# Two-layer transformer kernel on one core: the second attention's q and k projected once, the rotary partner fetched by transfers

## What is computed

```python
def rotate_half(x):
    half = x.shape[-1] // 2
    x1, x2 = (x[..., :half], x[..., half:])
    return jnp.concatenate([-x2, x1], axis=-1)

def apply_rope(x, base=BASE):
    ...
    emb = jnp.concatenate([freqs, freqs], axis=-1)
    return x * jnp.cos(emb) + rotate_half(x) * jnp.sin(emb)

q = (x @ q_w.T + q_b).reshape(B, S, H, Dh).transpose(0, 2, 1, 3)
k = (x @ k_w.T + k_b).reshape(B, S, H, Dh).transpose(0, 2, 1, 3)
q = apply_rope(q)
k = apply_rope(k)
attn = jnp.einsum('bhqd,bhkd->bhqk', q, k) * scaling
```

## Time and profile before

| | |
|---|---|
| time, median of 3 runs (lowest to highest) | 868.04 us (867.67 to 874.63) |
| span of the profiled execution | 863.3 us |
| the profiled execution's own time | not recorded; the median is 4.7 us above the span |
| TensorE busy | 828.1 us (96%), 4549 matmuls |
| VectorE, ScalarE, GpSimd busy | 646.3 (75%), 525.3 (61%), 465.8 us (54%) |
| granted TensorE clock, mean | 0.994 |
| projections of q and k, layer 1 | 96 matmuls, 493 to 623 us |

### The profile page before, as it was taken

The page is one execution under the profiler, slowest core; times in us unless marked ns, Lnnn a source line. Parts: engine busy times, 40 slices in busy tenths (PEclk is TensorE's granted clock), DMA queues, the critical chain, the costliest instruction groups (busy, mean ns, idle before and its releaser), DMA issues.

```text
span 863.3 us, 14805 instructions
## 1 busy us (share of the span) xinstructions
PE 828.1 (96%) x4549; PEld 627.4 (73%) x4549; DVE 646.3 (75%) x1350; ACT 525.3 (61%) x1106; POOL 465.8 (54%) x399
## 2 busy tenths in 40 slices
PE   8899999999989999989998999999999999999997
PEld 6678788777878888766887887764444447888886
DVE  5898888999998888998376865868788634676553
ACT  3778788787867888863644533336576554454442
POOL 4565555666665556551666776623300426656774
PEclk9999999999999999999999999999999989999999
DMA  4222222322422223122665357412441132334442
GB/s 157 93 98 87 98 97 97 106 81 87 152 74 99 98 97 110 61 69 60 208 210 182 131 163 275 138 57 73 137 136 51 57 99 93 123 123 142 152 162 65
DMA packets 57426, 99.20 MB, mean 115 GB/s; under 512 B 8272, under 2 KB 19024, under 8 KB 57360
## 3 DMA queue, kind: packets, MB, share of 16 engines
q1 hardware_dynamic: 57360, 98.39, 34.3%
HBM read 71.88 MB, written 9.57 MB: 94 GB/s over the span
## 4 chain that ended last, share of the span: by engine, by line
PE 64%; issue 10%; POOL 10%; DVE 10%; ACT 4%; DMA 2%; SPq 0%; DVEq 0%; POOLq 0%; ACTq 0%
PE ps L974 10%; PE ps L951 10%; PE ps L960 9%; PE ps L319 6%; PE ps L382 5%; PE ps L330 4%; POOL q_sin L526 3%; PE ps L343 3%; PE ps L370 3%; PE ps L1642 2%; PE ps L1523 2%; PE ps L357 2%; PE ps L1612 2%; POOL wqk_lo L513 2%; DVE nm L1834 2%
## 5 line engine op out<-in xcount | busy, mean ns | idle before, releaser
L1098 POOL TENSOR_TENSOR ew_lo<-ew_raw,ew_hi 128x768 fp32r<-128x768 f32 x68 | 128.6, 1892 | 56.7 <-ACT ew_hi L1064 48.5
L1050 ACT ACTIVATE hid_hi<-guw 128x512 fp32r<-128x512 f32 x68 | 43.0, 632 | 156.2 <-POOL guw L1114 106.2
L1153 DVE TENSOR_TENSOR hid_lo<-guw,hid_hi 128x512 fp32r<-128x512 f32 x68 | 78.9, 1160 | 72.4 <-ACT hid_hi L1050 72.3
L1114 POOL TENSOR_TENSOR guw<-gu,cwb 128x512 f32<-128x512 f32 x61 | 80.4, 1318 | 92.4 <-issue 76.4
L526 POOL TENSOR_TENSOR q_sin<-q_sw,sin 128x512 f32<-128x512 f32 x64 | 83.5, 1312 | 51.7 <-DMA q_sw<-q_in 50.4
L1834 DVE TENSOR_REDUCE nm<-ps 128x1 f32<-128x512 f32 x128 | 81.4, 683 | 19.0 <-PE ps L1546 17.8
L1729 ACT ACTIVATE e<-ps 128x512 f32<-128x512 f32 x128 | 68.7, 602 | 35.6 <-PE ps L1642 35.3
L974 PE MATMUL ps<-ew_hi,hid_hi 128*128 128x256 f32 x272 | 78.3, 288 | 2.4 <-DVE hid_lo L1153 1.8
L505 DVE SCALAR_TENSOR_TENSOR w<-ex,rden,sgn 128x512 f32<-128x512 f32 (+3 forms) x128 | 79.0, 680 | 0.0
L433 ACT ACTIVATE ex<-sabs,nmax 128x512 f32<-128x512 f32 (+3 forms) x128 | 61.5, 551 | 28.1 <-DVE nmax L479 28.1
L974 PE MATMUL ps<-ew_lo,hid_hi 128*128 128x256 f32 x272 | 76.8, 282 | 0.0
(11 more groups left out here) (189 smaller groups left out, 2401.6 us busy)
## 6 DMA issues: line engine op xcount, KB each, us to landing
ew_raw<-in_ew SPq DMA_DIRECT2D x68, 384.0 KB, 3.3
q_sw<-q_in SPq DMA_DIRECT2D x128, 128.0 KB, 2.0
cwb<-cw_dram SPq DMA_DIRECT2D x61, 256.0 KB, 3.7
wqk_raw<-in_wqk SPq DMA_DIRECT2D x32, 256.0 KB, 2.6
wv_raw<-in_wv SPq DMA_DIRECT2D x32, 128.0 KB, 2.4
wo_raw<-in_wo SPq DMA_DIRECT2D x32, 128.0 KB, 2.2
qs<-stk_q SPq DMA_DIRECT2D x16, 256.0 KB, 3.5
ks<-stk_k SPq DMA_DIRECT2D x16, 256.0 KB, 4.1
```

The source lines that it names most:

```text
L1098: pool.tensor_tensor(ff[f].ew[1][:, i % EW_SLOTS, :], ew_raw[:, i % RAW_SLOTS, :], fp(ff[f].ew[0][:, i % EW_SLOTS, :]), ALU.subtract).then ...
L1114: pool.tensor_tensor(ff[f].guw[:, i % 2, :], ff[f].gu[:, i % 2, :], ff[f].cwb[:, r % CWB_SLOTS, :], ALU.mult).then_inc(sem("guw"), 1)
L1153: dve.tensor_tensor(ff[f].hid[1][:, i % 2, :], ff[f].guw[:, i % 2, :], fp(ff[f].hid[0][:, i % 2, :]), ALU.subtract).then_inc(sem("hid_lo"), 1)
```

## The change

The plain weights alone are loaded, split and used: 48 projection matmuls instead of 96. The split of a weight writes the channels of a head in another order, the two halves interleaved, so that a channel and its rotary partner are neighbouring rows. Scores are sums over a head's channels, so the order is free as long as q and k share it. The tables and biases are loaded with the same order.

For each group ScalarE now evicts the projection with its bias (`evict`), SP issues two transfers that exchange odd and even rows (`swap_halves`), GpSimd multiplies by the signed sine (`turned`), VectorE makes the cosine part from PSUM after the eviction (`group_dve`), and the sum is made on VectorE in the rows and on GpSimd in the steps (`rotated`). The order of the queues and the places of groups, high halves, stores and loads change with it.

```diff
-        w1_raw = sb("w1_raw", [P, 6, DC, D])
+        w1_raw = sb("w1_raw", [P, 4, DC, D])
...
-        ROW_GROUP = {21: ((0, 0), (0, 1)), 22: ((1, 0), (1, 1)), 23: ((2, 0), (2, 1)), 24: ((3, 0),), 25: ((3, 1),)}
+        ROW_GROUP = {21: 0, 22: 1, 23: 2, 24: 3}
         ROW_V = {25: 0, 26: 1}
-        ROW_HIGH = {22: 0, 23: 1, 24: 2, 26: 3}
+        ROW_HIGH = {22: 0, 23: 1, 24: 2, 25: 3}
...
-        ROW_STACK = {23: 0, 24: 1, 26: 2, 27: 3}
-        ROW_LOADS = {25: (0, 4), 29: (4, SLOTS)}
+        ROW_STACK = {23: 0, 24: 1, 25: 2, 26: 3}
+        ROW_LOADS = {25: (0, 4), 28: (4, SLOTS)}
...
-        STEP_GROUP = {(4, 1): (4, 0), (4, 3): (4, 1), (5, 1): (5, 0), (5, 3): (5, 1), (7, 2): (6, 0), (8, 2): (6, 1),
-                      (9, 3): (7, 0), (10, 3): (7, 1)}
-        STEP_HIGH = {5: 4, 6: 5, 9: 6, 11: 7}
+        STEP_GROUP = {(4, 1): 4, (5, 1): 5, (7, 2): 6, (8, 2): 7}
+        STEP_HIGH = {6: 4, 7: 5, 9: 6, 10: 7}
...
-        W1_AT = {11 + 2 * part: part for part in range(5)}
+        W1_AT = {11 + 2 * part: part for part in range(3)}
...
+        def swap_halves(sp, g):
+            sp.wait_ge(sem("qk1_ev"), g + 1)
+            wait(sp, "rs", g - 1)
+            for o in range(2):
+                sp.dma_start(qw[o:P:2, g % 2, :], qe[1 - o:P:2, g % 2, :]).then_inc(sem(f"qk1_sw{g % 2}"), 16)
...
-            if i in ROW_STACK:
-                stack(sp, ROW_STACK[i])
...
+            if i in ROW_STACK:
+                stack(sp, ROW_STACK[i])
+            if i in ROW_GROUP:
+                swap_halves(sp, ROW_GROUP[i])
...
             loads_after(sp, 0)
+            swap_halves(sp, 4)
+            swap_halves(sp, 5)
             maxima(sp, 2)
             stack(sp, 4)
             stack(sp, 5)
             sp.wait_ge(sem("stk_st"), 16 * 3 * 6)
+            swap_halves(sp, 6)
             loads_after(sp, 1)
+            swap_halves(sp, 7)
             maxima(sp, 3)
             stack(sp, 6)
+            stack(sp, 7)
             loads_after(sp, 2)
-            stack(sp, 7)
             maxima(sp, 4)
...
+        def evict(act, g):
+            t, mt, h = GROUPS1[g]
+            act.wait_ge(sem("qk1_ps"), g + 1)
+            if g == 0:
+                act.wait_ge(sem("tab1"), 16 * 7)
+            wait(act, f"qk1_sw{g % 2}", 32 * (g // 2))
+            act.activation(qe[:, g % 2, :], ps[:, BANK_OF["qk", g], :], ACT.Identity,
+                           bias=b1[:, 2 * t, mt:mt + 1]).then_inc(sem("qk1_ev"), 1)
...
             if i in ROW_HIGH:
                 high(act, ROW_HIGH[i])
+            if i in ROW_GROUP:
+                evict(act, ROW_GROUP[i])
...
+                for j in range(HEADS):
+                    if (s, j) in STEP_GROUP:
+                        evict(act, STEP_GROUP[s, j])
                 if s in STEP_HIGH:
                     high(act, STEP_HIGH[s])
...
+        def turned(pool, g):
+            pool.wait_ge(sem(f"qk1_sw{g % 2}"), 32 * (g // 2 + 1))
+            wait(pool, "rr", g - 1)
+            pool.tensor_tensor(rs[:, g % 2, :], qw[:, g % 2, :], sin1[:, :], ALU.mult).then_inc(sem("rs"), 1)
...
-            if i in ROW_GROUP and ROW_GROUP[i][-1][1] == 1:
-                rotated(pool, ROW_GROUP[i][-1][0])
+            if i in ROW_GROUP:
+                turned(pool, ROW_GROUP[i])
...
             for g in range(4, 8):
+                turned(pool, g)
                 rotated(pool, g)
-                low(pool, g)
+                if g % 2 == 1:
+                    low(pool, g - 1)
+                    low(pool, g)
...
-        def group_dve(dve, g, sw):
+        def group_dve(dve, g):
...
+            dve.wait_ge(sem("qk1_ev"), g + 1)
...
+            dve.scalar_tensor_tensor(out=rc[:, g % 2, :], in0=ps[:, BANK_OF["qk", g], :],
+                                     scalar=b1[:, 2 * t, mt:mt + 1], in1=cos1[:, :],
+                                     op0=ALU.add, op1=ALU.mult).then_inc(sem("qk1_cos"), 1)
...
-                for g, sw in ROW_GROUP.get(i, ()):
-                    group_dve(dve, g, sw)
+                if i in ROW_HIGH:
+                    rotated(dve, ROW_HIGH[i])
+                if i in ROW_GROUP:
+                    group_dve(dve, ROW_GROUP[i])
```

88 lines of the change are left out of this document (47 added, 41 removed).

## The result

The changed kernel takes **875.57 us** (median of 20 runs, 870.74 to 884.02); the kernel before, on the same chip, 867.84 (20 runs, 862.40 to 876.82). The ratio is 1.0095, 95% interval 1.007 to 1.012: **slower by some 8 us**, where 2.7 us less were forecast. The profiled execution took 873.37 us, with a span of 871.2 for 863.3, and a mean granted clock of 0.984 for 0.994.

A forecast was written before the change was run, and what follows sets the result against it. TensorE, 96% busy, was taken as the bound, except for a chain of transfers before step 9. The terms -5.6 + 0.5 - 0.3 + 4.9 - 3.2 + 1.0 = -2.7 us gave a median of 865.3 us, range 858 to 873.

The forecast's parts named there:

- Rows, -5.6: Rows 21 to 24: four swapped projections go from a chain that is TensorE's alone, 4 x 1.40 = -5.6 us.
- What comes in their place, +0.5: Rows 21 to 24: eviction, exchange, sine product and sum run late but mostly covered, +0.5 us, bounds 0 and +2.5.
- The cycle: Rows 21 to 24: evict, swap, product, sum, high half and signalling for one group, 6.4 us against a 5.6 us row.
- the cover: Rows: slack, about 3.6 us, since GpSimd's weighting is used two rows later and gates wait for earlier low halves.
- The chosen bound, +2.5: Rows 21 to 24: the upper bound given for the +0.5 us cost of what replaces the swapped projections.
- Norm, -0.3: Ahead of the norm: fewer weight loads and splits shorten the chain there, -0.3 us, bounds -0.6 and 0.
- Release at step 9, +4.9: Attention steps 4 to 8: later maxima and group 5's store delay the stacked k reload to 619.9 from 614.95, +4.9 us.
- Group 7's projections, -3.2: Attention steps 9 to 13: group 7's two projections go, -3.2 us.
- Load at step 13, +1.0: Quad 2's loads, behind the stores of groups 6 and 7, land late for TensorE: +1.0 us, bounds 0 and +4.
- The rival of the stores: Rows and step 13: swaps and reload wait behind stacked stores, landings over some 6 us; +2.2, 870.2 us, chance 0.20.
- three quarters of TensorE's saving: TensorE loses 12.0 us of work; three quarters of it come back as waiting at steps 9 and 13.
- The 4.7 us: Whole kernel: median run 868.04 us less profiled span 863.3, taken as constant.

The follow-up runs named there:

- no_exchange: The changed kernel without the exchange transfers, the sine multiplying the unexchanged projection (values wrong); 869.79 us, ratio 1.0053 to the kernel before.
- before_loads_late: The kernel before with one edit: the load of the second quad's rows issued behind the store of group 7; 876.06 us, ratio 1.0131.
- no_exchange_early: The changed kernel without exchange transfers, group 5 projected at the end of step 4, second quad's load ahead of group 7's store; 863.3 us, ratio 0.9952.
- combined_swap6: The kernel combined with group 6's exchange put back ahead of the loads and ahead of the wait for the stores; 864.51 us, ratio 0.9987.
- combined: The changed kernel with rows' evictions and exchanges earlier, group 5 earlier, quad loads ahead of group 7's store and group 6's exchange; 870.83 us, ratio 1.0054.
- sine_on_vector: The changed kernel with the sine product of groups 0 to 3 moved from GpSimd to VectorE, just ahead of the sum; 876.03 us, ratio 1.0105.

## Why the prediction was wrong

Where the waits would come was seen; they were sized too short, and what they do to the clock was missed. By the prediction's own steps, with what the runs showed:

1. *Rows, -5.6*: right. With the exchange out the stretch is 5.6 us shorter.
2. *What comes in their place, +0.5*: **mis-sized, 3.3 us**. The cycle was put at 6.4 us and ran at 7.0 to 8.4. VectorE's sum took 1.76, the upper bound that I had passed over for 0.8, since it runs beside GpSimd's weighting, and the third swap took 4.1 us for 2.7. And the cover was misjudged: I looked for the lateness in the down products of two rows later, but it comes through ScalarE, where the gate's eviction of row 24 stands behind the high half. The chosen bound, +2.5, was under it as well.
3. *Norm, -0.3*: can't be told from the scatter of the stretch ahead of it.
4. *Release at step 9, +4.9*: right, +5.4, with some luck in the size. The maxima cost step 7 a wait of 0.6 us for 1.2 and the store's first issue came 0.7 us sooner than walked (counted from the first score), but from there to completion it took 8.2 us (605.38 to 613.59) for 7.3. And 2.5 us of it need no exchange at all, as no_exchange shows.
5. *Group 7's projections, -3.2*: 16.82 us became 14.28, so -2.5.
6. *Load at step 13, +1.0*: **mis-sized, 2.4**. The load of k was issued at 630.60 for the 628.4 that I walked to, and landed 6.5 us later behind both stores.
7. **The missing step**: each wait was entered at its own length. The granted clock of 0.50 behind the waits is in no term. It costs 2.1 + 2.5 = 4.6 us in the profiled execution, and 2.8 for one wait in the cleanest pair of traces. The warning was at hand in the trace of before. Every stretch that I printed had a clock of 1.00; behind a wait of 2.19 us in layer 0 it is 0.51 (TensorE's timeline, then the window, columns as above):

```profile
241.65 1.58 PE L357 MATMUL ps<-ident,w 128*128 128x128 f32 x10 [2.19 <-DVE w L505]
```

```profile
243.00:246.00 3.00, 3.00 (x15) 2.92 (x14) 3.00 (x7) 2.39 (x7) 0.73 (x1) 0.51 0.00 0
```

Together: 2.8 + 0.5 + 0.7 + 1.4 + 4.6 and 0.8 of noise ahead of row 21 are 10.8 us, for the 10.6 between -2.7 and +7.9. The rival of the stores had the right sign (870.2) and named the right places, rows and step 13, but its own mark, a landing of over 6 us, isn't met in the changed kernel's rows (3.9 us at most), and it lacked the clock too. That three quarters of TensorE's saving would come back as waiting was right in kind; with the clock, more than all of it came back. The 4.7 us that I took as constant between span and time are no such thing (about 2 us in each run of either kernel); as the forecast is a difference, they cancel.

Not tried: groups 0 to 3 with the exchange and 4 to 7 with two projections.

## What to carry to other kernels

Price a wait of TensorE twice: its length, and the slower clock behind it, which here cost 2.1 to 2.8 us for each of four waits between 1.4 and 7.2 us. A change that takes work off TensorE and lengthens a chain that was just hidden (0.6 us of waiting in 860) loses until the chain's order is redone with it: here one load moved ahead of one store, one exchange ahead of a wait, one group half a step earlier, and idle matmuls in what was left. Even then the 12 us of matmuls taken off brought nothing that these runs can tell from zero. And when an engine's queue holds an operation that waits for a round trip, ask what stands behind it on that queue; twice in this case, in the change and in my repair of it, it was the reading of a PSUM bank that TensorE needed.

## What the runs showed of the hardware

- The clock fell to 0.50 behind idle times of TensorE as short as 1.4 us (before_loads_late, 614.02) and 2.4 us, and in most traces it stayed there for 3 to 7 us of work, in no_exchange_early for 19.5 (to 630.9) behind a wait of 2.46. It did not fall behind each: waits of 2.29 us (the changed kernel, 521.80) and 2.24 us (combined_swap6, 550.43) left it at 1.00. Behind a wait that idle matmuls filled it did not fall in any of the six kernels that had them. The Trainium skill ("TensorE: Matmul & The Clock Gate", "What's actually happening") says that the clock has these two levels and that the lower one belongs to an idle TensorE. The levels agree; the stretch of 12.00 us busy out of 12.00 at 0.50 in combined doesn't, and there the measurement stands.
- VectorE's sum of two tensors in SBUF takes longer beside a GpSimd operation. In the changed kernel's rows it took 1763 ns on average. In sine_on_vector two sums started inside a GpSimd operation and ended 0.55 us behind its end, after 2.23 and 1.67 us; the third started with GpSimd idle and took 0.69. The Trainium skill ("GPSIMD Engine Reference", "Specifications") names contention of the two engines when VectorE reads two tensors of SBUF; these rows agree.

```profile
501.11 2.23 DVE L1819 TENSOR_TENSOR rr<-rc,rs 128x512 f32<-128x512 f32 x1
507.94 1.67 DVE L1819 TENSOR_TENSOR rr<-rc,rs 128x512 f32<-128x512 f32 x1
517.25 0.69 DVE L1819 TENSOR_TENSOR rr<-rc,rs 128x512 f32<-128x512 f32 x1
```

```profile
500.49 2.30 POOL L1098 TENSOR_TENSOR ew_lo<-ew_raw,ew_hi 128x768 fp32r<-128x768 f32 x1
507.29 1.77 POOL L1114 TENSOR_TENSOR guw<-gu,cwb 128x512 f32<-128x512 f32 x1 [4.50 <-issue]
...
514.82 1.84 POOL L1098 TENSOR_TENSOR ew_lo<-ew_raw,ew_hi 128x768 fp32r<-128x768 f32 x1
```

- Each of an exchange's two transfers (128 KB) lands in 1.9 to 2.1 us at its quickest and in 5.4 to 6.7 us behind a store.
- The mean clock of one kernel's runs scatters between 0.976 and 1.000 (the kernel before), and its time with it, 860 to 878 us: a difference of 1% needs some ten runs of each.
